# Another order of work in the slots with a quad: scores ahead of values, the fourth values product a slot later

## The chip, the cores and the metric

The kernel runs on one core of one Trainium2 chip. The metric is the device time of one execution in microseconds (us). TensorE does matmuls and transposes, ScalarE activations and copies out of PSUM, VectorE elementwise work and reduces, GpSimd (POOL) the indirect DMAs and a few powers, SyncE (SP) issues most of the other DMAs. Each engine works through its own list of instructions in order; engines wait for each other by semaphores.

## What is computed

One block of a gated cross-attention layer with a mixture of experts, for 64 sequences of 128 rows of 128 numbers, each with 77 context rows; 16 heads of depth 8; 8 experts with 256 hidden units, of which each row uses its best 2.

```python
q, k, v = layernorm(x) @ wq.T, ctx @ wk.T, ctx @ wv.T          # split into 16 heads
x = x + tanh(g_xattn) * (softmax(q k.T / sqrt(8)) v)
y = layernorm(x)
logits = y @ Wr + br;  gates = softmax over the 2 largest of 8
h = relu(y @ W1[e] + b1[e])
x = x + tanh(g_ffn) * sum over e of gates[e] * (h @ W2[e] + b2[e])
```

## The kernel before

The work is written as a pipeline of slots. In slot t every engine runs its own function slot(t), and sequence t enters; what is done for a sequence comes at fixed lags behind. In slot t the row maxima of scores are made for sequence mx = t - 8 (four head groups: max_scores on TensorE into one bank, head_max on VectorE, L1062), the scores, exponentials and values products for sequence sc = t - 13, and the outputs of sequence ob = t - 14 are turned, normed and added. scores(sc, h) (L523) fills one of two score banks, exp_scores(sc, h) (L772) on ScalarE empties it into probs, and values(sc, h) (L537) multiplies probs by V into bank_oT; h runs over four head groups. When all four values products are in, output_rows (L766) copies bank_oT to oT, and turn_o (L550) transposes oT into the bank o, from which VectorE norms. A scores product waits for the exponential two before it.

Four sequences make a group g. With r = t mod 4 the steps of a group are spread over the slots: r = 0 brings project_k (L460, which waits for the copy xT2 of an older group), the older group's second turned maxima (turn_max, L511) and the router (route, L561); r = 1 turn_x1 (L466); r = 2 project_q (L471) and the first turned maxima; r = 3 project_v (L476) and turn_x2 (L486). The copies out of PSUM for these (k_high, q_high, turned_x1, v_columns, turned_x2, turned_max) are on ScalarE. The router's product shares max_bank with max_scores and waits until head_max has read it.

The experts: rows of a chunk of 12 (the last 8) sequences are ranked by expert, scattered by indirect DMA into tiles of 128 rows of one expert each, and four tiles make a quad. A fixed schedule, worked out when the program is built, gives each of 38 quads a slot: 43 to 50, 55 to 62, 67 to 73, 75, 78 and then 79 to 91. In its slot a quad's hidden layer is made in two halves, hidden_part(q, 0) and (q, 1) (L611 to L613, twelve bf16 products each, weights named by registers), each waiting for ScalarE's relu of the half before (L838, four instructions). In the slot after, rows_out (L625, L627) makes the outputs in two halves; when both are in, outputs(q) (L847) copies the bank y on ScalarE, and in the slot after that store_y (L856) issues the store from ScalarE's queue. GpSimd gathers the stored rows and VectorE adds them. The last 8 sequences go through all experts without ranking, in slots 81 to 101.

In a slot with a quad and the outputs of another the lists are as follows. TensorE: [turn_max]; scores 0; max 0; [project_k or project_q]; hidden half 0; scores 1; max 1; turn_o; [route]; outputs half 0; values 0; scores 2; max 2; outputs half 1; [turn_x1 or project_v]; values 1; scores 3; max 3; values 2; hidden half 1; [turn_x2]; values 3. ScalarE: [turned_max]; output_rows; store_y; exp 0; [k_high or q_high]; relu half 0; exp 1; outputs; exp 2; [turned_x1 or v_columns]; exp 3; relu half 1. VectorE reduces maxima 0, 1, 2, 3 between other steps, the third behind the norm of the turned outputs.

Of the kernel before, what the change touches and what calls it, by code (L numbers as in the profile page):

```python
# [32 lines left out]
def clip(n, top):  # L33
    return max(0, min(n, top))


def flamingo_kernel(nc, x, ctx_t, g_xattn, g_ffn, w_att_t, w_router, b_router, w1, b1, w2, b2, out):
# [68 lines left out]
    with ExitStack() as stack:  # L106
# [204 lines left out]

        def dense_at(s):
            return [n for n in range(len(DENSE_AT)) if DENSE_AT[n] == s]
# [132 lines left out]
        def _(pe):  # L446
# [43 lines left out]
            def max_scores(b, h):  # L490
                g = b // NB
                if b % NB == 0 and h == 0:
                    pe.wait_ge(s_qst[g % 3], 16 * (g // 3 + 1))
                    pe.wait_ge(s_kst[g % 3], 16 * PER * (g // 3 + 1))
                n = HG * b + h + 1 - (HG if b < NB else 1)
                if n > 0:
                    pe.wait_ge(s_max, n)
                if h == 2 and b % NB == 0 and g >= 3:
                    pe.wait_ge(s_logit, g - 2)
                mm(max_to(b, h)[:, 0:PER * KEYS], q_st[g % 3][:, h, seq_cut(b, S)],  # L500
                   k_st[g % 3][:, h, b % NB, :, :].rearrange("p j k -> p (j k)"), start=True, stop=True,
                   skip_group_check=True).then_inc(p_max, 1)
# [50 lines left out]
            def route(g, t):  # L553
                if g == 0:
                    pe.wait_ge(s_bias, 16 * 3)
                pe.wait_ge(s_max, clip(HG * (t - MAX_LAG) + 2, HG * B))
# [115 lines left out]

            def slot(t):
# [4 lines left out]
                if r == 0 and group_on(u - 3):  # L678
                    turn_max(u - 3, 1)
                if r == 2 and group_on(u - 2):  # L680
                    turn_max(u - 2, 0)
# [4 lines left out]
                if r == 0 and later_group(u - 1):  # L686
                    project_k(u - 1)
                if r == 2 and later_group(u - 1):
                    project_q(u - 1)
# [21 lines left out]
                if r == 1 and later_group(u - 1):  # L711
                    turn_x1(u - 1)
                if r == 3 and later_group(u - 1):
                    project_v(u - 1)
# [11 lines left out]
                if r == 3 and group_on(u - 4):  # L726
                    turn_x2(u - 4)
                for c in range(NC):
                    if t == RANKED[c]:
                        ranks(c)  # L730
                if active(sc):
                    values(sc, 3)
# [15 lines left out]
        def _(act):  # L748
# [138 lines left out]

            def slot(t):
# [20 lines left out]
                if r == 0 and group_on(u - 3):  # L909
                    turned_max(u - 3, 1)  # L910
                if r == 2 and group_on(u - 2):
                    turned_max(u - 2, 0)
                if active(ob):
                    output_rows(ob)
                for q in quads_at(t - 2):
                    store_y(q)
                for n in dense_at(t):
                    dense_relu(n)
                if active(sc):
                    exp_scores(sc, 0)  # L920
                if r == 0 and later_group(u - 1):
                    k_high(u - 1)
                if r == 2 and later_group(u - 1):
                    q_high(u - 1)
                for q in quads_at(t):
                    name_biases(q)
                    relu(q, 0)
                if active(sc):
                    exp_scores(sc, 1)
# [53 lines left out]
        def _(dve):  # L983
# [296 lines left out]
            def slot(t):  # L1280
# [19 lines left out]
                if r == 2 and later_group(u - 1):  # L1300
                    q_low(u - 1)
                if r == 0 and group_on(u - 5):
                    make_logits(u - 5)
# [3 lines left out]
                if active(mx):  # L1307
                    head_max(mx, 2)
# [215 lines left out]
```

## Time and profile before

| | |
|---|---|
| median of 3 runs | 634.58 us (627.59, 634.58, 635.36) |
| the profiled execution | 634.84 us, span 633.1 us |
| mean granted TensorE clock | 0.956 of full speed |
| TensorE matmul busy | 556.7 us (88%) |
| VectorE, ScalarE, GpSimd busy | 369.5, 356.5, 272.7 us |

The span runs from the first to the last instruction. Busy shares are means over stages that differ, so the stretches of single slots are read too; a stretch's TensorE clock is a share of full speed, 1.00 being 2.4 GHz and 0.50 being 1.2 GHz.

### The profile page before, as it was taken

What the parts mean: (1) busy time and instruction counts of PE and PEld (TensorE: products, weight loads), DVE (VectorE), ACT (ScalarE), POOL (GpSimd) and SP (SyncE); (2) the same over time, 40 slices, a digit from 0 to 9 for tenths busy, and PEclk for the clock granted to TensorE, in tenths of its full rate; (3) what the DMA queues carried; (4) which work ended last, traced back from release to release, by engine and by line L of the source; (5) the groups of instructions that cost most, each with busy time, mean ns of one, the idle gap of its engine ahead of it and who ended that gap; (6) DMA issues with size and microseconds to landing.
All of it is one profiled execution on the core that took longest, in us unless ns stands there. A gap on an engine that the chain in (4) does not pass through costs nothing.

```text
span 633.1 us, 18491 instructions
## 1 busy us (share of the span) xinstructions
PE 556.7 (88%) x6213; PEld 399.3 (63%) x6213; DVE 369.5 (58%) x1361; ACT 356.5 (56%) x834; POOL 272.7 (43%) x283
## 2 busy tenths in 40 slices
PE   3579988999799889899889989999898879999996
PEld 1335555555455567767566767656676658898875
DVE  4466866878977864444865555785554324324364
ACT  2126756656566666656666566666655446656441
POOL 7430001000376003444464344673545456676771
PEclk9858989979999999999999899999999769999999
DMA  4936635634555657554788654495432526685431
GB/s 132 162 93 158 145 102 141 149 95 140 132 162 151 114 109 129 122 95 151 92 171 123 152 105 124 121 160 100 114 85 81 100 60 163 152 151 160 111 109 53
DMA packets 158121, 78.65 MB, mean 124 GB/s; under 512 B 85088, under 2 KB 153312, under 8 KB 158032
## 3 DMA queue, kind: packets, MB, share of 16 engines
q1 hardware_dynamic: 119760, 45.65, 34.2%
q10 hardware_dynamic: 31104, 17.13, 9.9%
q0 software_dynamic: 7168, 14.69, 9.5%
q8 instruction: 54, 0.88, 0.6%
q14 instruction: 35, 0.29, 0.2%
HBM read 30.72 MB, written 36.75 MB: 107 GB/s over the span
## 4 chain that ended last, share of the span: by engine, by line
PE 61%; DVE 12%; DMA 7%; issue 7%; ACT 6%; SPq 2%; ACTq 2%; POOL 2%; another core or an unknown queue 0%; DVEq 0%
PE y L627 13%; PE bank_oT L537 7%; PE scores L523 7%; DVE neg_max L1062 4%; PE max_scores L500 4%; PE hidden_p L611 4%; DMA q_st<-q_dram 3%; PE hidden_p L612 3%; PE max_scores L561 3%; PE o L550 2%; ACT probs L772 2%; DMA q_dram<-q_hl 2%; PE hidden_p L613 2%; PE bank_oT L668 2%; PE group L471 2%
## 5 line engine op out<-in xcount | busy, mean ns | idle before, releaser
L1062 DVE TENSOR_REDUCE neg_max<-max_scores 128x4 f32<-128x308 f32 x244 | 116.1, 476 | 128.9 <-PE max_scores L500 125.1
L772 ACT ACTIVATE probs<-scores 77x512 f32<-77x512 f32 x256 | 148.8, 596 | 50.3 <-PE scores L523 47.8
L1413 POOL DMA_INDIRECT xs_dram<-rows,at x112 | 109.8, 981 | 83.4 <-PE max_scores L500 51.3
L1428 POOL DMA_INDIRECT back<-ys_dram,at x112 | 107.6, 960 | 63.8 <-PE max_scores L500 26.8
L537 PE MATMUL bank_oT<-probs,v_cols 77*9 77x128 f32 x2048 | 104.2, 279 | 9.2 <-ACT probs L772 8.1
L523 PE MATMUL scores<-q_st,k_st 128*77 128x128 bf16 x1024 | 106.9, 229 | 0.3
L523 PEld LDWEIGHTS scores<-q_st,k_st 128*77 128x77 bf16 x1024 | 73.1, 119 | 47.5 <-issue 40.8
L838 ACT ACTIVATE hidden<-hidden_p,b_cols 128x128 f32<-128x128 f32 x256 | 73.6, 374 | 42.6 <-PE hidden_p L613 35.6
L627 PE MATMUL y<-w_sb,hidden 128*128 x608 | 95.0, 296 | 0.0
L500 PE MATMUL max_scores<-k_st,q_st 128*128 128x308 bf16 x244 | 75.4, 309 | 20.5 <-DVE neg_max L1062 12.3
L627 PEld LDWEIGHTS y<-w_sb,hidden 128*128 128x128 f32 x608 | 83.5, 199 | 2.4
L847 ACT COPY ys<-y 128x512 f32<-128x512 f32 x38 | 22.3, 587 | 75.4 <-PE y L627 75.4
L611 PE MATMUL hidden_p<-xsT,w_sb 128*128 128x128 bf16 x256 | 53.6, 229 | 11.5 <-ACT hidden L838 11.2
L1374 POOL TENSOR_TENSOR rstd<-ve,power 128x4 f32<-128x4 f32 x16 | 17.6, 1102 | 105.2 <-DVE ve L1030 105.1
L537 PEld LDWEIGHTS bank_oT<-probs,v_cols 77*9 77x9 f32 x2048 | 30.5, 88 | 50.8 <-ACT probs L772 21.6
L1368 POOL TENSOR_TENSOR rstd<-ve,power 128x4 f32<-128x4 f32 x16 | 17.1, 1068 | 94.4 <-DVE ve L1003 75.9
L613 PE MATMUL hidden_p<-xsT,w_sb 128*128 128x128 bf16 x256 | 53.1, 224 | 0.0
L612 PE MATMUL hidden_p<-xsT,w_lo 128*128 128x128 bf16 x256 | 52.8, 223 | 0.1
L766 ACT COPY oT<-bank_oT 128x512 f32<-128x512 f32 x64 | 37.6, 587 | 13.3 <-PE bank_oT L537 13.2
L500 PEld LDWEIGHTS max_scores<-k_st,q_st 128*128 128x128 bf16 x244 | 24.2, 99 | 32.9 <-DVE neg_max L1062 23.7
L550 PE MATMUL o<-ident,oT 128*128 128x128 f32 x256 | 40.4, 282 | 3.5 <-ACT oT L766 3.3
L611 PEld LDWEIGHTS hidden_p<-xsT,w_sb 128*128 x256 | 25.3, 99 | 27.8 <-issue 23.4
(160 smaller groups left out, 919.3 us busy)
## 6 DMA issues: line engine op xcount, KB each, us to landing
ys_dram<-ys ACTq DMA_DIRECT2D x38, 256.0 KB
q_st<-q_dram SPq DMA_DIRECT2D x16, 512.0 KB, 4.7
k_st<-k_dram SPq DMA_DIRECT2D x64, 77.0 KB
xs_all<-x SPq DMA_DIRECT2D x16, 256.0 KB, 4.2
q_dram<-q_hl SPq DMA_DIRECT2D x16, 256.0 KB
xs_dram<-zeros_b ACTq DMA_DIRECT2D x16, 256.0 KB, 3.0
out<-xs_all SPq DMA_DIRECT2D x16, 256.0 KB
k_dram<-k_hl SPq DMA_DIRECT2D x48, 77.0 KB
```

Source lines behind the costliest of these rows:

```text
L500: mm(max_to(b, h)[:, 0:PER * KEYS], q_st[g % 3][:, h, seq_cut(b, S)], k_st[g % 3][:, h, b % NB, :, :].rearrange("p j k -> p (j k)"), start ...
L523: last = mm(score_bank[h % 2][0:KEYS, j * S:(j + 1) * S], k_st[g % 3][:, h, b % NB, j, :], q_st[g % 3][:, h, seq_cut(b, S)], start=True, s ...
L537: last = mm(oT_bank[ROWS * j:ROWS * j + VW, h * S:(h + 1) * S], v_cols[g % 3][:, b % NB, h * PER + j, :], probs[h][:, j * S:(j + 1) * S], ...
L611: mm(o, w_hi[:, at_w], tiles[:, 0, cut], start=True, stop=False, skip_group_check=True)
L612: mm(o, w1_lo[:, at_w], tiles[:, 0, cut], start=False, stop=False, skip_group_check=True)
L613: last = mm(o, w_hi[:, at_w], tiles[:, 1, cut], start=False, stop=True, skip_group_check=True)
L627: last = mm(o, hidden[:, (2 * q + t // 2) % 4, t % 2, m, :], w2_sb[:, bass.ds(w + m * 128, 128)], start=False, stop=(m == HC - 1), skip_gr ...
L772: nc.scalar.activation(probs[h][:], score_bank[h % 2][0:KEYS, :], ACT.Exp, scale=SCALE).then_inc(s_exp, 1)
L838: last = nc.scalar.activation(hidden[:, k % 4, i, m, :], of[:, j * 128:(j + 1) * 128], ACT.Relu, bias=b1_cols[:, bass.ds(held[q][2 * half ...
L1062: V.tensor_reduce(neg_max[:, i // 2, :, h, i % 2], max_to(b, h)[:, 0:PER * KEYS].rearrange("p (j k) -> p j k", j=PER), AXIS_X, ALU.max, ne ...
L1413: G.indirect_dma_start(out=xs_dram[c % 2], out_offset=bass.IndirectOffsetOnAxis(ap=at[k][c % 4][:, i:i + 1], axis=0), in_=rows[c % 2][:, i ...
L1428: G.indirect_dma_start(out=back[k][:, b % 16, :], out_offset=None, in_=ys_dram[c % 2][0:TILES[c] * 128, :], in_offset=bass.IndirectOffsetO ...
```

## The change

It takes effect in slots t up to 78 that have a quad at t or at t - 1 (early_scores). There TensorE runs a list of its own, slot_of_quads; ScalarE and VectorE are reordered to match. The order on TensorE is now: scores 0; max 0; scores 1; values 3 of the sequence before; [turn_max]; [project_k or project_q]; max 1; hidden half 0; scores 2; max 2; values 0; turn_o; [route]; outputs half 0; scores 3; values 1; [turn_x1 or project_v]; outputs half 1; max 3; values 2; hidden half 1; [turn_x2]; values 3 only if the next slot is not such a slot. On ScalarE: exp 0; store_y; output_rows; exp 1; [turned_max]; [k_high or q_high]; relu half 0; then outputs, exp 2, exp 3 and relu half 1 as before. On VectorE head_max 2 goes ahead of the logits, the routing and the norm of the turned outputs. The router waits for the third maximum of the slot's sequence instead of the second, and the product that overwrites its columns, which waits for the logits, is the fourth instead of the third. Other slots keep their lists, with three exceptions: turn_max goes behind scores 0 and max 0 on TensorE, the copy of the turned maxima goes behind output_rows, store_y and exp 0 on ScalarE, and a slot whose next slot is one of the reordered leaves values 3 to it.

```diff
+        def early_scores(t):
+            return bool(quads_at(t) or quads_at(t - 1)) and t <= LAST_ATT
+
+        def values_behind(b, t):
+            return active(b) and not early_scores(t + 1)
...
-                if h == 2 and b % NB == 0 and g >= 3:
+                if h == (3 if early_scores(b + MAX_LAG) else 2) and b % NB == 0 and g >= 3:
                     pe.wait_ge(s_logit, g - 2)
...
-                pe.wait_ge(s_max, clip(HG * (t - MAX_LAG) + 2, HG * B))
+                pe.wait_ge(s_max, clip(HG * (t - MAX_LAG) + (3 if early_scores(t) else 2), HG * B))
...
+            def slot_of_quads(t):
+                u, r = t // NB, t % NB
+                mx, sc, ob = t - MAX_LAG, t - SCORE_LAG, t - OUT_LAG
+                if active(sc):
+                    scores(sc, 0)
+                if active(mx):
+                    max_scores(mx, 0)
+                if active(sc):
+                    scores(sc, 1)
+                if active(ob):
+                    values(ob, 3)
+                older_maxima(t)
+                first_group_step(t)
+                if active(mx):
+                    max_scores(mx, 1)
+                for q in quads_at(t):
+                    hidden_part(q, 0)
+                if active(sc):
+                    scores(sc, 2)
+                if active(mx):
+                    max_scores(mx, 2)
+                if active(sc):
+                    values(sc, 0)
+                if active(ob):
+                    turn_o(ob, t)
+                if r == 0 and group_on(u - 5):
+                    route(u - 5, t)
+                for q in quads_at(t - 1):
+                    rows_out(q, 0)
+                if active(sc):
+                    scores(sc, 3)
+                    values(sc, 1)
+                middle_group_step(t)
+                for q in quads_at(t - 1):
+                    rows_out(q, 1)
+                if active(mx):
+                    max_scores(mx, 3)
+                if active(sc):
+                    values(sc, 2)
+                for q in quads_at(t):
+                    hidden_part(q, 1)
+                last_group_step(t)
+                if values_behind(sc, t):
+                    values(sc, 3)
...
+                if early_scores(t):
+                    if active(sc):
+                        exp_scores(sc, 0)
+                    for q in quads_at(t - 2):
+                        store_y(q)
+                    if active(ob):
+                        output_rows(ob)
+                    if active(sc):
+                        exp_scores(sc, 1)
+                    older_maxima(t)
+                    first_group_step(t)
+                    for q in quads_at(t):
+                        name_biases(q)
+                        relu(q, 0)
+                else:
+                    if active(ob):
+                        output_rows(ob)
...
                 for q in quads_at(t - 1):
                     outputs(q)
                 if active(sc):
...
+                if early_scores(t) and active(mx):
+                    head_max(mx, 2)
                 if r == 0 and group_on(u - 5):
                     make_logits(u - 5)
                 routing(t, 0)
                 if active(ob):
                     heads_normed(ob)
-                if active(mx):
+                if not early_scores(t) and active(mx):
                     head_max(mx, 2)
```

older_maxima, first_group_step, middle_group_step and last_group_step hold the steps that stood in slot(t) under the same conditions: the turned maxima; project_k or project_q (k_high or q_high on ScalarE); turn_x1 or project_v; turn_x2 and the ranks.

## Rows read from the trace of the kernel before

**Rows 1.** Page, part 1: busy time and share of the span, TensorE's line and the others

```profile
PE 556.7 (88%) x6213; PEld 399.3 (63%) x6213; DVE 369.5 (58%) x1361; ACT 356.5 (56%) x834; POOL 272.7 (43%) x283
```

**Rows 2.** Page, part 4: the chain that ended last, by engine

```profile
PE 61%; DVE 12%; DMA 7%; issue 7%; ACT 6%; SPq 2%; ACTq 2%; POOL 2%; another core or an unknown queue 0%; DVEq 0%
```

**Rows 3.** Busy time by stretch: length, busy of each engine, TensorE clock, DMA

```profile
224.21:235.08 10.87, 9.51 (x111) 7.14 (x111) 5.62 (x20) 6.12 (x17) 0.33 (x1) 1.00 0.42 65
235.08:244.42 9.34, 8.57 (x110) 6.46 (x106) 5.41 (x20) 5.97 (x17) 0.70 (x1) 1.00 0.86 92
244.42:253.38 8.96, 8.58 (x103) 6.26 (x103) 4.15 (x14) 5.67 (x17) 5.27 (x6) 1.00 0.63 179
253.38:263.34 9.96, 9.21 (x117) 7.22 (x113) 4.54 (x18) 6.46 (x18) 3.92 (x5) 1.00 0.70 139
354.68:365.95 11.27, 10.54 (x118) 8.56 (x114) 5.76 (x22) 6.46 (x18) 3.50 (x4) 0.85 0.59 125
224.21:292.31 68.10, 62.28 (x749) 46.89 (x748) 32.79 (x116) 42.09 (x112) 24.07 (x25) 1.00 0.59 118
325.45:394.79 69.34, 63.34 (x748) 48.20 (x748) 37.52 (x132) 42.02 (x112) 31.73 (x33) 0.98 0.59 125
427.80:483.36 55.56, 49.98 (x615) 37.78 (x614) 29.75 (x108) 33.15 (x90) 25.41 (x26) 1.00 0.41 96
```

**Rows 4.** TensorE's waits between 211 and 484 us: total, times, longest

```profile
PE hidden_p L611 <- ACT hidden L838: 7.2, 10, 0.8
PE bank_oT L537 <- ACT probs L772: 5.2, 14, 0.5
PE group L460 <- ACT xT L805: 2.8, 3, 1.0
PE max_scores L500 <- DVE neg_max L1062: 2.6, 9, 0.4
PE o L511 <- DVE nm_hl L1072: 1.8, 3, 0.6
```

**Rows 5.** Chain between 227 and 268 us: start, length, what

```profile
231.82 0.51 PE y L627 x4
...
233.48 0.41 PE bank_oT L537 x8
...
234.74 0.07 PE hidden_p L613
...
236.34 0.23 PE hidden_p L611
...
237.64 0.22 PE scores L523 x4
237.86 0.13 PE max_scores L500
...
239.88 0.35 PE scores L523 x4
...
242.73 0.34 PE bank_oT L537 x8
243.07 0.16 PE hidden_p L611
...
243.87 0.06 PE hidden_p L613
...
266.70 0.49 DVE neg_max L1062
```

**Rows 6.** ScalarE's timeline in slot 45: start, length, instruction, idle before

```profile
241.52 0.59 ACT L847 COPY ys<-y 128x512 f32<-128x512 f32 x1 [2.13 <-PE y L627]
242.00 0.59 ACT L772 ACTIVATE probs<-scores 77x512 f32<-77x512 f32 x1
```

**Rows 7.** Busy time by stretch, behind slot 76

```profile
499.36:506.32 6.96, 6.96 (x42) 6.04 (x40) 2.39 (x12) 0.43 (x1) 1.45 (x2) 0.51 0.79 108
509.80:520.00 10.20, 7.23 (x53) 6.45 (x52) 3.71 (x14) 3.55 (x12) 6.47 (x7) 0.51 0.27 76
```

More of the change, by code:

```diff
@@ L671, in dense_out, with older_maxima, first_group_step @@
                 last.then_inc(p_dy, 1)
+            def older_maxima(t):
+                u, r = t // NB, t % NB
+                if r == 0 and group_on(u - 3):
+                    turn_max(u - 3, 1)
+                if r == 2 and group_on(u - 2):
+                    turn_max(u - 2, 0)
+            def first_group_step(t):
+                u, r = t // NB, t % NB
+                if r == 0 and later_group(u - 1):
+                    project_k(u - 1)
+                if r == 2 and later_group(u - 1):
+                    project_q(u - 1)
@@ new lines, in middle_group_step, with last_group_step @@
+            def middle_group_step(t):
+                u, r = t // NB, t % NB
+                if r == 1 and later_group(u - 1):
+                    turn_x1(u - 1)
+                if r == 3 and later_group(u - 1):
+                    project_v(u - 1)
+            def last_group_step(t):
+                u, r = t // NB, t % NB
+                if r == 3 and group_on(u - 4):
+                    turn_x2(u - 4)
+                for c in range(NC):
+                    if t == RANKED[c]:
+                        ranks(c)
@@ L677, in slot @@
                     name_weights(q)
[L678 to L681, printed above, removed]
+                if early_scores(t):
+                    slot_of_quads(t)
+                    return
                 if active(sc):
@@ L710, in slot @@
                     rows_out(q, 1)
[L711 to L714, printed above, removed]
+                middle_group_step(t)
                 if active(sc):
@@ L725, in slot @@
                     hidden_part(q, 1)
[L726 to L731, printed above, removed]
+                last_group_step(t)
+                if values_behind(sc, t):
                     values(sc, 3)
@@ L886, in dense_relu, with older_maxima, first_group_step @@
                                          bias=b1_cols[:, j:j + 1]).then_inc(s_drelu, 1)
+            def older_maxima(t):
+                u, r = t // NB, t % NB
+                if r == 0 and group_on(u - 3):
+                    turned_max(u - 3, 1)
+                if r == 2 and group_on(u - 2):
+                    turned_max(u - 2, 0)
+            def first_group_step(t):
+                u, r = t // NB, t % NB
+                if r == 0 and later_group(u - 1):
+                    k_high(u - 1)
+                if r == 2 and later_group(u - 1):
+                    q_high(u - 1)
             def slot(t):
@@ L908, in slot @@
                     b2_part(t - 16)
[L909 to L929, printed above, removed]
+                if early_scores(t):
+                    if active(sc):
[6 more added lines that the diff above has]
+                        exp_scores(sc, 1)
+                    older_maxima(t)
+                    first_group_step(t)
+                    for q in quads_at(t):
[4 more added lines that the diff above has]
+                        output_rows(ob)
+                    for q in quads_at(t - 2):
+                        store_y(q)
+                    for n in dense_at(t):
+                        dense_relu(n)
+                    if active(sc):
+                        exp_scores(sc, 0)
+                    older_maxima(t)
+                    first_group_step(t)
+                    for q in quads_at(t):
+                        name_biases(q)
+                        relu(q, 0)
+                    if active(sc):
+                        exp_scores(sc, 1)
                 for q in quads_at(t - 1):
```

5 lines of the change are left out of this document (1 added, 4 removed).

## The prediction

> **What bounds the kernel now.** The page comes first: TensorE is busy for 88% of a span of 633.1 us [rows 1], and of the chain that ended last 61% is TensorE's, 12% VectorE's, 7% "issue" and 6% ScalarE's [rows 2]. So the kernel is as long as TensorE's list of instructions with the holes in it. The profiled execution took 634.84 us, 1.7 more than its span, and the median of the three runs is 634.58, so I work against 634.84 as if it were the median. The runs spread from 627.59 to 635.36; 2% (12.7 us, so 621.9 and 647.3) is about what a measurement here tells from no change.
>
> Next come the slots that the change rewrites. The start of scores(sc, 0) in the timeline marks a slot's start. Twenty slots have a quad's hidden layer and the outputs of the quad before it: 44 to 50, 56 to 62 and 68 to 73. The reader sees in [rows 3] how long four neighbours are (10.87, 9.34, 8.96, 9.96 us for t mod 4 = 0, 1, 2, 3) and how long the three blocks are (68.10, 69.34, 55.56), with TensorE busy for 90 or 91% of each. The other changed slots are 43, 55, 67 and 75 (hidden layer alone), 51, 63, 74 and 76 (outputs alone), and 78, where no sequence is in attention any more.
>
> Then the holes. Between 211 and 484 us TensorE waits 10 times for the relu before a hidden layer, 14 times for an exponential before a values product, 3 times for xT before a K projection, 9 times for a reduce before a max product, and 3 times for the maxima's halves before turn_max [rows 4]. The chain shows the two that matter, piece by piece [rows 5]. Hole one, in odd slots and in slots 69, 70, 71 and 73: the first half of the hidden layer starts at 236.34 though the half before it had ended at 234.81 (234.74 + 0.07); these 1.53 us are the relu and its hand-over, and values(3), scores(0) and max(0) fill some of it. Hole two, in even slots and in all of 68 to 73: outputs(q-1) stands on ScalarE ahead of exp(2), so values(2) starts at 233.48, 1.15 us after the last output product (231.82 + 0.51 = 232.33). [rows 6] shows that order: the copy of y waited 2.13 us for TensorE, and the exponential follows it 0.48 later. In odd slots up to 63 turn_x1 or project_v, values(1), scores(3) and max(3) lie in those 1.15 us, and nothing is seen of them.
>
> **The change part by part.** Nothing is removed or added in work; the matmuls, reduces, copies and DMAs are the same, so only holes change.
>
> *Values(2).* New order: scores(3) and values(1), and turn_x1 or project_v, are issued ahead of the second half of the outputs; between its end and values(2) only max(3), 0.13, is left. ScalarE's list from outputs on is as before, so exp(2) still can't start before the copy of y. The hole becomes 1.15 - 0.13 = 1.02 in each slot that has outputs. Before, it was in even slots 1.15 less values(1) 0.34, scores(3) 0.35 and max(3) 0.13: 0.33, as the waits' 5.2 us over 14 times also say (0.37). So +0.69 in even slots and in all six of the last block, +1.02 in odd slots of the first two. Queued behind it on TensorE are the second half of the hidden layer, turn_x2 and the ranks; relu(q, 1) waits for the first of these, and the next slot's hidden layer for that relu: the loss goes on down the chain whole.
>
> *Hidden layer's wait.* Before, values(3) 0.34, scores(0) 0.35 and max(0) 0.13 filled 0.82 of the 1.53, which leaves 0.71; the waits' 7.2 us over 10 times say 0.72. After, scores(0) 0.22, max(0) 0.13, scores(1) 0.22, values(3) 0.34 and max(1) 0.13 plus 0.10 (next paragraph) fill 1.14 and leave 0.39: -0.32 in odd slots and in 69, 70, 71 and 73. In slots with t mod 4 = 2 of the first two blocks project_q covers it (the ten waits are all in other slots), before and after: 0. In slots with t mod 4 = 0 the K projection waits for xT in both orders, and scores(1) alone moves into that wait: -0.22.
>
> *Pieces.* A scores product is 0.35 behind values and 0.22 behind a bf16 product; scores(0), (2) and, if the fp32 outputs leave no mark, (3) go from the first to the second, -0.26 to -0.39 a slot. Against it, a product behind values can cost 0.10 more (the first hidden product there is 0.16, others 0.06), and three values products now stand before other products than scores: 0 to +0.30. Ends -0.39 and +0.04; I take -0.10, near their middle (-0.17), as none of these neighbours is seen in the trace; 0 in slots with t mod 4 = 0 of the first two blocks, where the cheaper scores(0) only lengthens the wait for xT.
>
> *Router.* It now waits for the third reduce, 0.49 (the last row of [rows 5]), with K's low half ahead of it on VectorE, but values(0) and turn_o lie between: 0 to +0.49, I take +0.15, in slots with t mod 4 = 0 of the first two blocks, as K's half is there alone.
>
> *What moves beside the path, at nothing.* output_rows, store_y with its DMA and the turned maxima's copy go behind exp(0) or exp(1) on ScalarE, which idles 2.13 us later in the slot [rows 6]; the turned maxima's copy, behind three pieces of 0.48 more, reaches SP's queue some 1.4 us later, and they are needed three slots later; q's high half, behind one piece more and a later project_q, about 1 us later, feeds a store and a stack on SP's queue that are needed two slots (some 18 us) later; y's store is needed by the gathers of a whole chunk. Were that cover gone, each would cost its delay once a slot. POOL's pacing counts max products, and these move by parts of a us. VectorE's third reduce ahead of the logits has room in both orders.
>
> *Sum for a slot*: t mod 4 = 0: 0.69 - 0.22 + 0.15 = 0.62; 1 and 3: 1.02 - 0.32 - 0.10 = 0.60; 2: 0.69 - 0.10 = 0.59. Two blocks of seven: 2 x (2 x 0.62 + 3 x 0.60 + 2 x 0.59) = 8.4. Last block: 6 x (0.69 - 0.10) - 4 x 0.32 = 2.3. Slots 51 and 63 (no wait before, 1.02 after, less 0.10): 1.8. Slots 74 and 76, which have no second project or turn to cover it either, as in the last block: 2 x 0.59 = 1.2. Slots 43, 55, 67: max(3) waits there for a third reduce that stands behind the turned outputs, and no longer will; a wait for a reduce is 0.29 (2.6 over 9): -0.9. *Other slots.* turn_max goes behind scores(0) and max(0) in all slots, on ScalarE behind exp(0). The three waits of 0.6 for the maxima's halves are in slots 42, 54 and 66, where 0.35 + 0.13 now goes ahead of it: -1.4. The copy on ScalarE is needed by turn_o only, behind project and two more pairs of products: nothing.
>
> Together 8.4 + 2.3 + 1.8 + 1.2 - 0.9 - 1.4 = +11.4, so **646.2 us**.
>
> A rule of the Trainium skill speaks for a better end. The rows first: behind the wait for the relu the twelve hidden products run from 236.34 to 237.64, 1.30 us, behind the wait of values(2) from 233.89 (233.48 + 0.41) to 234.81, 0.92, and behind the unwaited values(2) from 243.07 to 243.93, 0.86. "TensorE: Matmul & The Clock Gate", section "Architectural detail", says that TensorE's queue is deep and pulls weight loads ahead of running products. By it a longer wait would let the queue fill, and the products behind it would run close; the rows show the slowest products just behind the waits, so the sum is made by the rows. By the rule the time is rival (1)'s.
>
> **The rivals.** (1) *The queue fills in the longer wait.* Then the hidden layer behind it goes at its pace without a wait. At best that is 0.86 for 1.30 in the ten slots of hole one (-4.4), 0.92 to 0.86 in ten others (-0.6), and the scores and values pieces at their cheap end, -0.39 in place of -0.10, in twenty slots (-5.8): -10.8; with the products of 0.16 at 0.06 twice a slot besides (-4.0) it is -14.8, and the time 631.4, not slower than before. It decides from 11.4 us recovered, 0.57 in each of the twenty. Against it: the rows just named. For it: "issue" is 7% of the chain. (2) *The clock falls more often.* Slot 59 took 11.27 at a granted 0.85, slot 47 with the same work 9.96 at 1.00 [rows 3]: one fall to 1.2 GHz cost 1.31, and it followed hole two and hole one in a slot like all others. The new hole two is thrice as long; if the clock fell in seven of the twenty slots, that is +9.2: 655.4. For it: one fall has been seen at shorter holes; against it: nineteen slots with the same holes have none. (3) *The falls of before don't come back.* At 499.36 to 506.32 and 509.80 to 520.00 the clock is at about half, with TensorE busy 6.96 and 7.23 [rows 7]: at 2.4 GHz about half of that goes, 7.1, or only the first stretch's 3.5 where relus wait anyway. These stretches begin in slots 76 to 78, whose order around the turned outputs changes. Middle 5.3: 640.9. (4) That the change does nothing would need TensorE off the path in these slots; [rows 2] and [rows 3] speak against it, and I give it no chance of its own.
>
> **How the numbers follow.** Forecast 0.62, its own range 640 to 650 (the pieces' ends, -0.29 and +0.14 in twenty slots, are -5.8 and +2.8, and the router's upper end is +0.34 in four, 1.4). Rival (1) 0.10, (2) 0.13, (3) 0.15. The likeliest is the forecast, 646. For 8 in 10 I leave out rival (1) and the upper half of (2): 637 to 656. Slower by over 2% is over 647.3: four tenths of the forecast's 0.62, and (2), so 0.25 + 0.13, about 0.38; faster by over 2% is beyond what rival (1) gives, and I leave 0.03 for it; 0.59 lies between.
>
> **What would show it.** In the changed profile: values products' waits for exponentials of about 1.0 in each of twenty to twenty-four slots (some 22 us in all, from 5.2); waits before the hidden layer of 0.3 to 0.5 in place of 0.7; exp(2) 0.5 behind the copy of y, and that copy's own wait longer than 2.13; slots longer by about 0.6 each. It is wrong if the products behind the waits run close (rival 1), if rows at 1.2 GHz turn up in the quads' blocks (2) or are missing after them (3), or if the copy of y doesn't stand ahead of exp(2).

## The result and the profile after

The changed kernel takes 652.71 us (median of four runs, 649.33 to 657.54) against 634.03 for the kernel before on the same chip; the ratio is 1.032, with a 95% interval from 1.023 to 1.042. It is 18.7 us slower where 11.4 were forecast. The profiled execution took 653.19 us, with a span of 651.4. The time lies above the forecast's own range of 640 to 650 us and inside the 637 to 656 that it gave 8 chances in 10. Here and below the medians hold all executions, and the ratios and their intervals leave out those more than 1.5% above the fastest of the same kernel.

The page after, part 1 and the first line of part 4, to be read beside [rows 1, 2]:

```profile
PE 562.5 (86%) x6213; PEld 401.4 (62%) x6213; DVE 373.7 (57%) x1361; ACT 356.5 (55%) x834; POOL 271.8 (42%) x283
...
PE 62%; DMA 11%; DVE 10%; issue 7%; ACT 6%; SPq 2%; ACTq 1%; POOL 0%; DVEq 0%
```

The same number of matmuls is busy for 5.8 us more, and their share falls from 88 to 86%: TensorE's list has longer holes, and some of its products take longer. TensorE's waits between 211 and 500 us (us in all, times, longest), to be read beside [rows 4] (line numbers have moved by 6 on TensorE, by 70 on ScalarE and by 93 on VectorE):

```profile
PE bank_oT L543 <- ACT probs L842: 23.3, 23, 1.2
PE scores L529 <- issue: 2.7, 10, 0.3
PE max_scores L506 <- DMA q_st<-q_dram: 2.2, 2, 1.5
PE max_scores L506 <- DVE neg_max L1155: 1.9, 7, 0.4
...
PE scores L529 <- ACT probs L842: 1.1, 2, 0.5
...
PE hidden_p L617 <- ACT hidden L908: 0.3, 1, 0.3
```

The first line is the change: values products wait 23.3 us for exponentials in place of 5.2, 1.0 a time. The waits for the relu, 7.2 us before, are all but gone; two new lines, "issue" and exponentials ahead of scores products, have come in. The blocks of [rows 3] after (stretch and length, busy time of each engine, TensorE's clock, DMA):

```profile
223.93:297.07 73.14, 63.04 (x750) 47.33 (x749) 33.70 (x116) 42.35 (x113) 23.91 (x25) 1.00 0.57 113
331.12:406.31 75.19, 64.54 (x751) 48.45 (x750) 38.55 (x132) 42.51 (x113) 31.80 (x33) 0.98 0.54 118
440.07:498.83 58.76, 50.20 (x617) 38.03 (x616) 30.36 (x108) 33.75 (x91) 25.74 (x27) 1.00 0.38 94
```

They are longer by 5.04, 5.85 and 3.20 us, 14.1 together where the forecast had 10.7. The other 4.2 us of the two spans' difference of 18.3 lie around the blocks, where the forecast had 0.7. By slots, the scores(0) of slots 44 to 51 start at 223.93, 235.49, 245.47, 255.50, 265.96, 277.46, 287.44 and 297.07.

Slot 45 and the start of slot 46, TensorE, with most of the hidden and output products left out (start, length, instruction, idle before):

```profile
235.49 0.39 PE L529 MATMUL scores<-q_st,k_st 128*77 128x128 bf16 x4 [0.30 <-issue]
235.71 0.29 PE L506 MATMUL max_scores<-k_st,q_st 128*128 128x308 bf16 x1
235.84 0.39 PE L529 MATMUL scores<-q_st,k_st 128*77 128x128 bf16 x4
236.16 0.41 PE L543 MATMUL bank_oT<-probs,v_cols 77*9 77x128 f32 x8
236.58 0.30 PE L506 MATMUL max_scores<-k_st,q_st 128*128 128x308 bf16 x1
236.80 0.23 PE L617 MATMUL hidden_p<-xsT,w_sb 128*128 128x128 bf16 x1
...
242.63 0.29 PE L506 MATMUL max_scores<-k_st,q_st 128*128 128x308 bf16 x1
243.96 0.41 PE L543 MATMUL bank_oT<-probs,v_cols 77*9 77x128 f32 x8 [1.04 <-ACT probs L842]
244.29 0.23 PE L617 MATMUL hidden_p<-xsT,w_sb 128*128 128x128 bf16 x1
...
245.12 0.22 PE L619 MATMUL hidden_p<-xsT,w_sb 128*128 128x128 bf16 x1
245.47 0.39 PE L529 MATMUL scores<-q_st,k_st 128*77 128x128 bf16 x4
```

Max(3) and values(2), which start at 242.63 and 243.96 there, in slot 46 of the kernel before:

```profile
251.14 0.29 PE L500 MATMUL max_scores<-k_st,q_st 128*128 128x308 bf16 x1
251.78 0.41 PE L537 MATMUL bank_oT<-probs,v_cols 77*9 77x128 f32 x8 [0.35 <-ACT probs L772]
```

ScalarE's list in slot 45 of the changed kernel, beside [rows 6]:

```profile
242.83 0.59 ACT L917 COPY ys<-y 128x512 f32<-128x512 f32 x1 [3.45 <-PE y L633]
243.31 0.59 ACT L842 ACTIVATE probs<-scores 77x512 f32<-77x512 f32 x1
```

The copy of y waits 3.45 us (2.13 before), the exponential follows it 0.48 later, and values(2) follows that 0.65 later, at 243.96. The scores(2) that this exponential reads were made from 237.94 on, within 0.4 us: it is late only because it stands behind the copy. From one second half of the hidden layer to the next first half (235.03, which is 234.97 plus 0.06, to 236.80) it is now 1.77 us, with no wait for the relu in it: a gap of about 0.46 and five groups of products fill the hand-over.

### The profile page after: what moved, and what is told of

Its sections match the earlier page's. It is cut to its first block, busy times and chain, and to the rows that moved or that the text cites. A ratio compares the mean times of both kernels' runs of the same rounds, so it can differ in the third digit from the quotient of the medians.

```text
span 651.4 us, 18491 instructions
## 1 busy us (share of the span) xinstructions
PE 562.5 (86%) x6213; PEld 401.4 (62%) x6213; DVE 373.7 (57%) x1361; ACT 356.5 (55%) x834; POOL 271.8 (42%) x283
## 4 chain that ended last, share of the span: by engine, by line
PE 62%; DMA 11%; DVE 10%; issue 7%; ACT 6%; SPq 2%; ACTq 1%; POOL 0%; DVEq 0%
PE y L633 12%; PE bank_oT L543 8%; DMA q_st<-q_dram 7%; PE scores L529 6%; PE max_scores L506 4%; ACT probs L842 4%; PE o L556 3%; PE hidden_p L617 3%; DVE neg_max L1155 3%; PE hidden_p L618 3%; PE max_scores L567 2%; DMA q_dram<-q_hl 2%; PE o L674 2%; PE bank_oT L674 2%; PE hidden_p L619 2%
## 5 line engine op out<-in xcount | busy, mean ns | idle before, releaser
L529 PE MATMUL scores<-q_st,k_st 128*77 128x128 bf16 x1024 | 103.7, 227 | 7.4 <-ACT probs L842 3.8
L529 PEld LDWEIGHTS scores<-q_st,k_st 128*77 128x77 bf16 x1024 | 77.5, 119 | 44.0 <-issue 33.4
L556 PE MATMUL o<-ident,oT 128*128 128x128 f32 x256 | 42.3, 290 | 2.3 <-issue 1.6
```

Of the source, the lines that this page charges most:

```text
L529: last = mm(score_bank[h % 2][0:KEYS, j * S:(j + 1) * S], k_st[g % 3][:, h, b % NB, j, :], q_st[g % 3][:, h, seq_cut(b, S)], start=True, s ...
```

## The experiments

Each is compared with the kernel before, run beside it on the same chip (median 635.73 us for the first four, 632.78 for the next four, 636.12 for the last two). A ratio is to that kernel, with its 95% interval in brackets; the views are TensorE's waits between 211 and 500 us, where nothing else is said. Nothing of the computation is left out or changed in any of them; one copies y once more than needed.

**The exponential ahead of the copy.** In ScalarE's slot of the changed kernel:

```diff
-                for q in quads_at(t - 1):
-                    outputs(q)
                 if active(sc):
                     exp_scores(sc, 2)
+                for q in quads_at(t - 1):
+                    outputs(q)
```

> The changed kernel with one edit on ScalarE: the third exponential ahead of the copy of y (in every slot). Theory A (the loss is the third values product waiting for an exponential that stands behind the copy of y): TensorE's waits for exponentials before values products, 23.3 us over 23 in the changed kernel, fall to under 2 us, and the time falls by 19 to 23 us from 652.7, to 630 to 634. Theory B (the loss is in the pieces and in the 0.3 to 0.5 us gaps behind the second hidden half, and the wait only moves to the next relu): the waits before the hidden layer rise by as much as these fall, and the time stays above 645.

Measured: 624.55 us, ratio 0.985 [0.977, 0.992]. Its waits:

```profile
PE scores L529 <- ACT probs L842: 4.4, 6, 1.7
...
PE hidden_p L617 <- ACT hidden L908: 3.0, 6, 1.4
...
PE bank_oT L543 <- ACT probs L842: 1.1, 2, 0.8
```

One instruction moved on ScalarE takes away 28 us, more than the whole loss. The values products' waits fall from 23.3 to 1.1, and two things go with them. The twelve products of a second hidden half behind values(2) run closer (slot 45, TensorE's timeline, first and last of them and the scores behind):

```profile
239.96 0.23 PE L617 MATMUL hidden_p<-xsT,w_sb 128*128 128x128 bf16 x1
...
240.58 0.22 PE L619 MATMUL hidden_p<-xsT,w_sb 128*128 128x128 bf16 x1
240.64 0.39 PE L529 MATMUL scores<-q_st,k_st 128*77 128x128 bf16 x4
```

They take 0.68 us, against 0.89 behind the wait, and so does every second half of the three blocks in this run (0.68 or 0.69); and scores(0) stands right behind them, without the gap. Of the 4.4 us that scores products wait for exponentials, 3.9 are ahead of scores(2) in slots 51, 63, 74 and 76 (0.57, 0.57, 1.09 and 1.69). These slots have the outputs of a quad and no hidden layer of their own, so nothing long stands between scores(0) and scores(2), and exp(0), which scores(2) needs, stands on ScalarE behind the relus of the slot before (in slot 76 behind two copies more). The changed kernel has the same four (0.51, 0.55, 1.12 and 1.61, the last two behind slot 73).

**The registers' loads later.** The gap ahead of scores(0) was put down to name_weights, which at the slot's head loads into registers the four numbers by which the quad's weights are addressed, and lay under values(3) before.

```diff
                 if active(ob):
                     values(ob, 3)
+                for q in quads_at(t):
+                    name_weights(q)
                 older_maxima(t)
```

(and taken from the head of these slots.)

> The changed kernel with one edit on TensorE: in the reordered slots the four register loads of the quad's weight addresses go from the head of the slot to behind the fourth values product. Theory A (the gaps of 0.3 to 0.5 us between the second hidden half and the next scores, 15 of them with 5.9 us in all, are these loads, which nothing covers any more since the fourth values product has left its place ahead of them): the gaps go, and the time falls by 4 to 6 us to about 647. Theory B (the gaps are the hidden products' own dispatch behind the wait): gaps and time stay, 652 to 653.

Measured: 650.53 us, ratio 1.025 [1.017, 1.034]. The gaps are gone from the waits, but the relu is back:

```profile
PE bank_oT L543 <- ACT probs L844: 23.0, 22, 1.2
...
PE hidden_p L617 <- ACT hidden L910: 3.0, 9, 0.7
```

So the loads make the gap, but in slots with t mod 4 = 1 and 3 and in the last block the relu's hand-over stands right behind it (0.2 to 0.3 us in most places), and about 2 us is all that is got back, within what the runs scatter.

**The order of before with the exponential first.** The same edit as in the first experiment, made on the kernel before.

> The kernel before with the same edit on ScalarE alone: the third exponential ahead of the copy of y. Theory A: its 14 waits for exponentials (5.2 us) go and the time falls by 4 to 6 us to 629 to 631. Theory B (these waits are slack that the next relu takes up): no change, 634.

Measured: 626.78 us, ratio 0.983 [0.973, 0.992] (one of the four executions took 2477 us; without it the median is 626.43).

```profile
PE hidden_p L611 <- ACT hidden L838: 7.5, 11, 0.9
...
PE bank_oT L537 <- ACT probs L772: 0.8, 2, 0.4
```

The values' waits go from 6.1 (5.2 up to 484 us, [rows 4]) to 0.8, the relu's stay at 7.5 as forecast; the gain, 9 us, is larger than the waits that went.

**The cover put back.** In the changed kernel scores(3), values(1) and turn_x1 or project_v go behind the second half of the outputs again; all else as changed.

```diff
                 for q in quads_at(t - 1):
                     rows_out(q, 0)
+                for q in quads_at(t - 1):
+                    rows_out(q, 1)
                 if active(sc):
                     scores(sc, 3)
                     values(sc, 1)
                 middle_group_step(t)
-                for q in quads_at(t - 1):
-                    rows_out(q, 1)
```

> The changed kernel with TensorE's third scores step, second values product and the x or V step put back behind the second half of the outputs, the rest as changed. Theory A: the wait before the third values product falls from 1.04 to about 0.35 in 14 slots and to nothing in the 8 that have a V or x step, 9.7 + 8.3 = 18 us less, about 635. Theory B (register loads, pieces and the clock): waits fall but the time stays above 645.

Measured: 633.46 us over ten runs, ratio 0.995 [0.991, 1.000].

```profile
PE bank_oT L543 <- ACT probs L842: 6.5, 16, 0.6
...
PE scores L529 <- issue: 2.8, 10, 0.5
```

The whole loss is gone by this move alone, from the other side than in the first experiment: not the exponential earlier, but the work that hides its lateness back in its place. The gaps of "issue" are as long as in the changed kernel (2.8 us for 2.7), and the time is that of before: they alone don't make it slow.

**Both exponentials ahead of the copy.** exp(3) too stands ahead of outputs(q).

```diff
                 if active(sc):
                     exp_scores(sc, 3)
+                for q in quads_at(t - 1):
+                    outputs(q)
```

> The new order with the copy of y on ScalarE behind exp(2) and exp(3) both. With exp(2) alone ahead of the copy the waits of TensorE for exponentials between 211 and 500 us were 1.1 us at values(2) and 4.4 us at scores(0) of the next slot, which needs the bank that exp(3) reads, and exp(3) stood behind the copy. Theory A (each hole is set by what stands ahead of the exponential on ScalarE): the 4.4 us go, the time falls by 2 to 4 us to about 621. Rival (the copy of y in its turn comes late: the outputs of the next slot wait for the bank of y, or the half hidden layer's relu behind it comes later): a new wait of the outputs or of the hidden layer for ScalarE of 3 us or more in all, time 624 or more.

Measured: 623.07 us, ratio 0.984 [0.978, 0.989].

```profile
PE scores L529 <- ACT probs L842: 3.9, 4, 1.6
...
PE bank_oT L543 <- ACT probs L842: 0.4, 2, 0.2
```

The expected step isn't there: the waits of scores for exponentials are 3.9 in place of 4.4, so most of them did not come from the copy, and the time can't be told from the first experiment's. The trace shows where they are: ahead of scores(2) in slots 51, 63, 74 and 76 (0.57, 0.57, 1.12 and 1.61), for exp(0), not ahead of scores(0) for exp(3) as the expectation had it. Only 0.4 us of the 4.4 lay elsewhere, and they are gone. The profiled execution is the longest of the seven (634.09 us, granted clock 0.943); the profile of the eighth experiment, of 614.98 us, has the same exponentials first and the same four waits:

```profile
PE scores L529 <- ACT probs L844: 3.9, 4, 1.7
```

**The turned maxima alone.** The order of before, with turn_max behind scores(0) and max(0), and its copy behind exp(0).

```diff
+                if active(mx):
+                    max_scores(mx, 0)
                 if r == 0 and group_on(u - 3):
                     turn_max(u - 3, 1)
                 if r == 2 and group_on(u - 2):
                     turn_max(u - 2, 0)
-                if active(mx):
-                    max_scores(mx, 0)
```

(scores(sc, 0) moves with it; on ScalarE likewise.)

> The order of before with one part of the change alone: turn_max behind scores(0) and max(0) on TensorE, its copy behind exp(0) on ScalarE, in all slots. The forecast put -1.4 us on this (waits of 0.6 in slots 42, 54 and 66). Theory A: the wait is moved and not removed, since in slots 44 and 56 a max product waits for the load of q whose store and load start from those same slots: the waits for the maxima's halves go, the wait for q_st in slots 44 and 56 grows by as much, time 0 to -0.5 us. Rival (forecast): -1.4 us, the wait for q_st as before (1.1 a time).

Measured: 634.06 us, ratio 1.004 [1.000, 1.008].

```profile
PE group L460 <- ACT xT L805: 3.4, 4, 1.0
...
PE o L550 <- ACT oT L766: 2.6, 2, 1.6
PE o L550 <- issue: 1.4, 5, 0.5
```

The waits for the maxima's halves are gone (1.8 us before, [rows 4]), the wait for the load of q in slot 56 as well, against the first theory's expectation; yet nothing is gained. In their place stand 1.4 us of "issue" ahead of turn_o and 0.6 more for xT; these are less than what went, and where the rest is was not found. The forecast's -1.4 us is refuted in this order (the interval begins at 1.000), and so is the story that the load of q takes it.

**The fourth values product back.** The changed kernel with values(3) at its own slot's end.

```diff
         def values_behind(b, t):
-            return active(b) and not early_scores(t + 1)
+            return active(b)
...
-                if active(ob):
-                    values(ob, 3)
                 older_maxima(t)
```

> The changed kernel with the fourth values product back at its slot's end, everything else as changed. Theory A (the 0.3 to 0.5 us of issue between the second half of the hidden layer and the next scores(0) are the register loads of name_weights, which values(3) covered before): the issue gaps ahead of scores(0) go (2.7 us between 211 and 500), but the relu before the next hidden layer then has less of scores and values ahead of it only by the place of values(3), which lies between the halves in both orders, so that the hand-over is filled as before: time 4 to 7 us below the changed kernel, about 647. Rival (the gap is hidden by the relu's hand-over of 1.53 us behind it, as with the loads moved alone): 0 to 2 us, about 651 to 652, with waits of the hidden layer for the relu of 3 us or more.

Measured: 655.16 us, ratio 1.041 [1.032, 1.049].

```profile
PE bank_oT L543 <- ACT probs L840: 23.3, 23, 1.2
PE max_scores L506 <- DVE neg_max L1153: 6.0, 19, 0.4
```

The gaps go, as expected, and nothing is gained: max products (in odd slots max(1), which loses values(3) ahead of it) wait for reduces in 19 places (6.0 us, from 1.9). Neither theory had this wait; the rival's time was the nearer one. The hole ahead of values(2) stands as it was, and putting the fourth product back takes nothing off the loss.

**Both exponentials first and the loads later.** The edits of the second and the fifth experiment together.

> The new order with both exponentials ahead of the copy of y and, besides, the loads of the weights' registers behind values(3) in place of the slot's head. Theory A (with no wait of values(2) TensorE's sequencer runs ahead and has the registers loaded before the products arrive): no difference to the kernel with the two exponentials first alone, within 1.5 us. Rival (the loads still hold up scores(0), 0.3 us in each of some 20 slots): 3 to 6 us faster than that kernel.

Measured: 620.16 us, ratio 0.982 [0.975, 0.988]. It is 2.9 us under the kernel without the later loads, between what the two expected, and the two intervals overlap. This is the lowest median of all and is clearly below both kernels; its first block shows what remains of the holes, 63.35 us where before had 68.10 and after 73.14:

```profile
219.82:283.17 63.35, 60.72 (x751) 46.50 (x750) 33.58 (x116) 42.76 (x113) 23.82 (x25) 1.00 0.64 126
```

**The order of before with both exponentials first.** The edit of the fifth experiment on the kernel before.

> The order of before on TensorE and VectorE, with exp(2) and exp(3) both ahead of the copy of y on ScalarE. The new order with the same two ahead took 0.9838 of before [0.9782, 0.9893], with the loads of the weights' registers later as well 0.9815. Theory A (once no values product waits behind the copy of y, the new order removes the 1.53 us hand-over ahead of the hidden layer as well, which the old order keeps): the waits of the hidden layer for the relu stay at about 7 us, the time at 626 or more, ratio 0.988 or more. Rival (the order is worth nothing by itself and all of the gain is the exponentials' place): 620 to 623, ratio about 0.981 to 0.985.

Measured: 625.7 us, ratio 0.984 [0.977, 0.990].

```profile
PE hidden_p L611 <- ACT hidden L838: 5.9, 9, 0.9
...
PE bank_oT L537 <- ACT probs L772: 0.7, 2, 0.4
```

The relu's waits stay, as the theory said, but the ratio is that of the new order with the same edit (0.984). So the new order is worth nothing that these runs can show once the exponentials come first. It takes away part of the relu's waits (2.5 us with the same edit) and brings the 3.9 us of scores(2); that the one pays for the other is argued from these two, not shown.

**The copy made twice.** The changed kernel with a second copy of y, into a buffer that nobody reads, ahead of the real one. It makes the wait for the real copy, and so the hole ahead of values(2), longer.

```diff
+                if q:
+                    act.wait_ge(s_twice, q)
+                copy(y_twice[:], y_bank[:]).then_inc(s_twice, 1)
                 copy(ys[q % 2][:].rearrange("p t d -> p (t d)"), y_bank[:]).then_inc(s_ys, 1)
```

> The changed kernel with the copy of y made twice by ScalarE (the first one into a buffer that nobody reads), so that the hole ahead of values(2) is longer by one copy, some 0.5 us, in each of 24 slots with outputs. Theory A (the hole stands whole on the path): the waits of values(2) grow from 1.04 to about 1.5 each, 23 us to 35 in all, and the time by 24 x 0.5 = 12 us, to 663 to 666; the gaps of 0.3 ahead of scores(0) stay. Rival (a longer wait lets the products behind it follow closer, or part of the hole is slack elsewhere): 4 to 8 us more, below 661.

Measured: 671.76 us, ratio 1.060 [1.052, 1.068], 19 us above the changed kernel, more than either expected. Its wait:

```profile
PE bank_oT L545 <- ACT probs L844: 30.6, 21, 1.5
```

Three of its slots by stretch (45, 47 and 49), in the columns of [rows 3], and then slot 49 of the changed kernel:

```profile
237.12:248.45 11.33, 9.68 (x105) 7.44 (x105) 5.73 (x22) 6.24 (x16) 1.36 (x2) 0.85 0.49 67
...
258.98:270.35 11.37, 9.85 (x115) 7.73 (x113) 4.65 (x18) 6.52 (x17) 4.95 (x5) 0.91 0.41 111
...
282.37:292.84 10.47, 8.78 (x105) 6.53 (x105) 4.72 (x18) 6.15 (x16) 4.72 (x5) 1.00 0.35 76
```

```profile
277.46:287.44 9.98, 8.78 (x104) 6.57 (x105) 4.72 (x18) 5.62 (x15) 4.22 (x5) 1.00 0.37 79
```

Slot 49 runs at full clock in both, and the 0.48 us by which its hole is longer (1.52 for 1.04) are in it whole (10.47 against 9.98): the products behind a longer wait run no closer. 24 times 0.49 is 11.8. The rest, some 7 us, was not split. Part of it goes with the clock, which in this kernel is below full speed in slots 45 (0.85), 46 (0.94), 47 (0.91) and 50 (0.94), where the changed kernel has 1.00; but in the second block (slots 56 to 62), with the same holes, it is 1.00.

## Why the prediction was right, point by point, and what it under-sized

**Values(2): right.** The forecast put 1.02 us ahead of values(2) in each slot with outputs; the trace shows 1.04 of idle time, four in a row alike, and 23.3 us in 23 waits. Start to start, from max(3) to values(2), it is 1.33 in slots 45 and 46. In slot 46 before it was 0.64, so +0.69 as forecast; in slot 45 0.22, so +1.11 for 1.02. The cause is shown from three sides: with the exponential ahead of the copy, or the cover back, the loss is gone; with the copy twice, a slot at full clock grows by the length of one copy.

**Hidden layer's wait: right in kind, too small.** Forecast was a wait of 0.39 in place of 0.71; there is almost none. In slot 45 the wait of 0.89 (from 235.45, the end of max(0)'s turn, to 236.34; the forecast's 0.71 counts from the end of max(0) itself) goes whole.

**Pieces: the step that failed.** The pieces are the small groups of scores, max and values products. The forecast took -0.10 a slot for them, between ends of -0.39 and +0.04. All of them in slot 45 added up start to start, without the waits and the hole, are 2.78 us before and 3.11 after: +0.33. In slot 46 the same sum is 2.72 and 2.92: +0.20. The rows of slot 45 show where: scores(1) to values(3) is 0.32 (235.84 to 236.16) where scores(0) to max(0) is 0.22, values(3) to max(1) 0.42, max(1) to the hidden layer 0.22 where scores(1) follows max(0) after 0.13. Not all of it is new. Before, values(0) stood behind the outputs, and that half of the outputs took 1.21 us in slot 45 where the other took 1.12; now all halves take 1.11 to 1.13, and the dearer step is counted with a scores or max product. With the row of outputs, turns and projection (less turn_max) the difference is +0.25 in slot 45 and +0.18 in slot 46, still outside both ends. The forecast had put the dearer neighbours at 0 to +0.30 and drawn them toward the gain.

**What it left out: the gap.** name_weights' loads, under values(3) before, stand bare between the second half of the hidden layer and scores(0): 0.29 ahead of slot 46, 0.45 ahead of slot 47 (255.05 to 255.50). The text called the moved work free and named what hid each; this one wasn't named. The second and the seventh experiment show that taking the gap alone away gains little, as other waits stand behind it.

**What it left out: scores(2) in slots 51, 63, 74 and 76.** There scores(2), which comes earlier in the new order, waits for exp(0): 0.51, 0.55, 1.12 and 1.61 us, which the forecast did not have. In part this replaces other waits of before: 0.35 for a reduce in slots 51 and 63, 1.0 and 1.6 for oT ahead of turn_o in slots 74 and 76.

The whole of two slots, from the timelines of both kernels (us):

| | slot 45 before, after | difference | slot 46 before, after | difference |
|---|---|---|---|---|
| max(3) to values(2) | 0.22, 1.33 | +1.11 | 0.64, 1.33 | +0.69 |
| wait ahead of the first hidden half | 0.89, 0 | -0.89 | 0, 0 | 0 |
| gap behind the second half | 0, 0.29 | +0.29 | 0, 0.45 | +0.45 |
| scores, max, values groups | 2.78, 3.11 | +0.33 | 2.72, 2.92 | +0.20 |
| hidden layer | 2.00, 2.03 | +0.03 | 1.88, 1.46 | -0.42 |
| output halves, turns, projection | 3.45, 3.22 | -0.23 | 3.72, 3.87 | +0.15 |
| slot | 9.34, 9.98 | +0.64 | 8.96, 10.03 | +1.07 |

(The groups' row leaves out max(3), which the first row has; the row of outputs, turns and projection holds turn_max, 0.15 to 0.17, which moves from the end of slot 45 into slot 46.) So slot 45 came out at +0.64 for a forecast of +0.60 by errors that cancel: pieces and gap 0.72 dearer, the relu's wait 0.57 cheaper, and turn_max's 0.15 gone from the slot. That its total is right is luck. Slot 46 has no relu wait to pay with, and came out at +1.07 for +0.59, with 0.17 of it turn_max.

**Router: right in the total, wrong in the term.** The three slots with t mod 4 = 0 at full clock, 44, 48 and 60, are longer by 0.69, 0.74 and 0.70 for 0.62. But the +0.15 for the router isn't in them: from turn_o to the router it is 0.51 us in slot 44 and 0.52 in slot 48, where before it was 0.74 and 0.73, so the router became 0.2 cheaper, and the gap of 0.45 us behind the second half, which the forecast did not have, makes up for it. **Slots 42, 54, 66: wrong.** The sixth experiment shows that -1.4 us isn't there: the waits go and others come. **Slots 43, 55 and 67, -0.9: wrong.** The forecast took the mean of the nine waits for reduces of [rows 4], but these nine lie in slots 51 to 53 and 63 to 65. Without turn_max the three slots take 6.82, 6.87 and 7.28 us before and 7.00, 6.95 and 7.02 after: nothing in all. **Slots 51 and 63**, with the slots behind them, grew by 1.57 and 1.80, of which 0.34 each is a values product that the order now leaves to them: 1.23 and 1.46 for 0.92. The wait of scores(2) is 0.16 and 0.20 longer than the wait for a reduce that it replaces; the rest was not split.

**The rivals.** (1), the queue filling in the longer wait, would have given 631.4. Behind the wait of 1.04 the twelve hidden products of slot 45 take 0.89 (244.29 to 245.18), and those of the three blocks 0.78 to 0.89; behind the waits of 0.35 before they took 0.79 to 0.88, and behind a values(2) without a listed wait 0.68 to 0.86. The copy made twice adds its whole length. They don't run closer behind a longer wait; they do where the wait is gone, 0.68 or 0.69 in the first experiment. The Trainium skill's rule ("TensorE: Matmul & The Clock Gate", section "Architectural detail"), that a deep queue pulls weight loads ahead of running products, gives nothing back behind these waits. (2), the clock falling more often, isn't seen in the blocks at this length of hole: their clocks are 1.00, 0.98 and 1.00 in both kernels, with one fall in slot 56 after (13.66 us at 0.88, for 10.94 before) where before had one in slot 59. It is seen once behind them: slot 74 stands at 0.83 where before it had 1.00, and takes 10.10 us for 7.47, the first two rows below (before, after). With holes of 1.5 us the tenth experiment has it in four slots of its first block and in none of its second, so the rival was near. (3), the falls behind slot 76 not coming back, is refuted by the stretch behind slot 74, the last two rows (before, after): about as long and at the same clock in both.

```profile
483.36:490.83 7.47, 5.97 (x85) 4.44 (x82) 3.38 (x15) 4.11 (x11) 3.95 (x5) 1.00 0.23 72
498.83:508.93 10.10, 7.62 (x85) 5.92 (x82) 3.15 (x14) 4.24 (x11) 4.32 (x5) 0.83 0.18 58
490.83:521.53 30.70, 24.41 (x235) 19.81 (x236) 8.92 (x37) 13.75 (x36) 14.65 (x15) 0.72 0.38 83
508.93:540.00 31.07, 24.22 (x243) 19.80 (x244) 9.15 (x38) 13.64 (x36) 14.93 (x15) 0.73 0.38 80
```

**The sum.** The blocks gave 14.1 for 10.7 and their surroundings 4.2 for 0.7. The first block, at full clock in both kernels, came out at 5.04 for 4.2. Its seven slots added up like the two of the table, by term (a wait counts as what a distance between two starts has over its usual length):

| slots 44 to 50 | forecast | measured |
|---|---|---|
| max(3) to values(2), the hole | +5.82 | +6.05 |
| wait for the relu | -0.96 | -2.70 |
| gap behind the second half | 0 | +1.94 |
| pieces, with outputs, turns, projections | -0.50 | +1.21 |
| hidden products | 0 | -0.78 |
| router | +0.30 | -0.56 |
| waits of slots 44 and 48 by the K projection | -0.44 | -0.35 |
| turn_max (that of slot 44 moves into the block) | 0 | +0.23 |

So the hole, which is the main term, was right; the gap and the pieces cost 3.65 us more than forecast, and the relu's wait, the hidden products and the router give 3.38 back. The mechanism was right, and that the block's total is so near is in part luck. The second block's 5.85 for 4.2 has the clock in it: slot 56 grew by 2.72, and slot 59 is 0.81 shorter. Around the blocks, up to slot 68 it is +1.4 for -0.5, as the savings of 1.4 and 0.9 did not come; behind slot 73 it is +2.8 for 1.2, and slot 74 with its lower clock has 2.63 of it. The other blocks were not split by terms.

## What to carry to other kernels

When a consumer's input is made late because of the order on another engine, reordering the consumer's engine only moves the cover: look first at what stands ahead of the producer, where one moved instruction was worth 9 us in the kernel before and 28 in the changed one, and a rewritten list beside it nothing that these runs show. When an order is changed, list for each wait what lies between its release and its use, and count register loads among the work that needs cover. When a product comes earlier in a list, check the slots that lack the work which covers its input elsewhere. Where a rearrangement gives products new neighbours, price each pair from a pair of that kind in the trace, and without one take the dear end.

## What the runs showed of the hardware that was not expected

A values product (fp32, 77 rows by 9 columns of weights) starts 0.32 us behind the start of a bf16 scores group, where a bf16 max product starts 0.22 behind it; behind a half of the outputs it costs about as much more (1.21 us in place of 1.12 in slot 45 before). Whether type or shape makes it was not tried. Register loads that name weights show as up to 0.34 us of "issue" ahead of the next product when nothing long stands in front of them (ten times in the changed kernel); they are gone with the loads behind values(3), and all but gone (0.2 us in all) where TensorE is not held up at values(2). A hole costs more than its length: the twelve hidden products behind it take 0.78 to 0.89 us, without it 0.68, which with the gap is part of why 22 us of waits taken away gave 28. Holes of 1.04 us in each slot left the clock at 1.00 in nearly all slots of the blocks. With holes of 1.5 us it stood at 0.85 to 0.94 in slots 45 to 47 and 50 and at 1.00 over the 77.18 us of the second block, so the length of the hole alone doesn't settle it.
